# Finishing each attention tile one tile later, three more warm-up runs of TensorE, and a reordered feed-forward tail

## The reference

```
x = x + cross_attention_0(layernorm(x), ctx)      # 16 heads, 16 batches, 1601 keys of width 256
x = x + state_space(layernorm(x), ...)            # gated Mamba-like scan, 16 heads, state 64
x = x + block_ffn(layernorm(x), ...)              # router softmax, top 4 of 16 blocks of 128, relu
x = x + cross_attention_1(layernorm(x), ctx)      # one head: softmax(q k^T) v, 64 queries x 1601 keys a batch
x = x + self_attention(layernorm(x), ...)         # causal, query width 64
x = x + quantised_ffn(layernorm(x), ...)          # weights rounded to 4 bits in blocks of 32

w_block -> s = max(|w_block|) / 7;  clip(round(w / s), -8, 7) * s      # the 4-bit weights
```

## Time and profile before

| | |
|---|---|
| median of 3 runs | 1714.09 us |
| profiled execution, own time / span | 1715.84 / 1714.1 us |
| PE, DVE, ACT, POOL busy | 91%, 68%, 52%, 45% |
| granted TensorE clock, mean | 0.965 of full |
| `state_space` | 851.3 to 993.9 us of the span |
| `block_ffn` | 993.9 to 1229.4 |
| `cross1_queries`, `cross1_batches` | 1229.4 to 1256.7, to 1407.7 |
| `self1`, `quant_ffn` | to the end, not touched |

### The profile page before, as it was taken

One profiled execution on the slowest core, in us unless ns is written; L12 is line 12 of the kernel. 1 busy time (PEld: TensorE's weight loads), 2 busy tenths in 40 slices (PEclk: granted clock), 3 DMA queues, 4 the chain that ended last, 5 costly groups with the idle time before them and its releaser, 6 DMA issues. The chain is left out here.

```text
span 1714.1 us, 33945 instructions
## 1 busy us (share of the span) xinstructions
PE 1559.1 (91%) x13873; PEld 813.7 (47%) x13982; DVE 1167.6 (68%) x1951; ACT 889.2 (52%) x1190; POOL 770.2 (45%) x384
## 2 busy tenths in 40 slices
PE   6999999999999999999799979978878989899469
PEld 3445555555555555555446453333534444444224
DVE  6688888888888888886646448987522233626981
ACT  1487777777777777776373025411211222326750
POOL 1477788888878887885204816642000000000000
PEclk9999999999999999999999969989999999999779
DMA  4589999999999999999713764558679935000001
GB/s 138 131 177 192 193 190 192 190 191 191 194 194 190 199 195 195 189 182 173 166 49 123 232 261 92 140 152 202 196 305 365 396 147 221 1 1 0 1 0 49
DMA packets 556678, 282.74 MB, mean 165 GB/s; under 512 B 482912, under 2 KB 534624, under 8 KB 553456
## 3 DMA queue, kind: packets, MB, share of 16 engines
q1 hardware_dynamic: 556528, 280.63, 69.0%
HBM read 138.74 MB, written 22.54 MB: 94 GB/s over the span
## 5 line engine op out<-in xcount | busy, mean ns | idle before, releaser
L572 POOL TENSOR_TENSOR x<-x_prob,x 128x1604 bf16<-128x1604 f32 x120 | 388.0, 3233 | 142.3 <-ACT x L737 142.3
L867 DVE TENSOR_REDUCE x_negmax<-x_score 128x1 f32<-128x1604 f32 x128 | 233.6, 1825 | 17.3 <-PE x_score L613 7.0
L727 ACT ACTIVATE x_prob<-x_score,x_negmax 128x1604 f32<-128x1604 f32 x128 | 204.8, 1600 | 25.8 <-DVE x_negmax L867 21.1
L596 PE MATMUL x_ring<-x_ctx_hi,wk_split 128*128 128x400 bf16 (+1 forms) x1024 | 216.2, 333 | 0.2 <-DVE x_kT L795 0.2
L596 PE MATMUL x_ring<-wv_split,x_ctx_hi 128*128 128x512 bf16 (+1 forms) x770 | 200.4, 379 | 9.6 <-issue 7.3
L795 DVE SCALAR_TENSOR_TENSOR x_kT<-x_ring,bk,x_kT 128x400 bf16<-128x400 f32 (+1 forms) x256 | 162.2, 634 | 31.8 <-ACT x_kT L716 23.8
L737 ACT CAST x<-x_prob 128x1604 bf16<-128x1604 f32 x120 | 182.9, 1525 | 0.0
L801 DVE TENSOR_TENSOR x_v<-x_ring,x_v 128x512 bf16<-128x512 f32 (+1 forms) x208 | 143.7, 691 | 52.9 <-ACT x_v L720 50.0
L716 ACT ACTIVATE x_kT<-x_ring,bk 128x400 bf16<-128x400 f32 (+1 forms) x196 | 116.3, 594 | 91.0 <-PE x_ring L596 90.0
L720 ACT CAST x_v<-x_ring 128x512 bf16<-128x512 f32 (+1 forms) x148 | 86.5, 585 | 96.8 <-PE x_ring L596 96.8
L596 PEld LDWEIGHTS x_ring<-x_ctx_hi,wk_split 128*128 128x128 bf16 x1024 | 93.9, 97 | 86.9 <-issue 19.7
(11 more groups left out here) (346 smaller groups left out, 2435.9 us busy)
## 6 DMA issues: line engine op xcount, KB each, us to landing
y_ctx<-in_ctx SPq DMA_DIRECT2D x16, 1664.0 KB, 10.4
y_ctxT<-in_ctxT SPq DMA_DIRECT2D x16, 1601.0 KB, 14.3
x_stage<-in_ctxT SPq DMA_DIRECT2D x48, 400.0 KB, 4.4
x_q_rows<-q_rows SPq DMA_DIRECT2D x64, 128.0 KB, 3.2
m_xT<-in_L_ffn_w SPq DMA_DIRECT2D x16, 512.0 KB, 4.5
ffn_w_parts<-m_xT SPq DMA_DIRECT2D x32, 256.0 KB, 2.6
x_stage<-in_ctxT SPq DMA_DIRECT2D x16, 401.0 KB, 5.0
f_w<-ffn_w_parts SPq DMA_DIRECT2D x4, 1024.0 KB, 8.5
```

What stands on the lines that cost most here:

```text
L572: pool.tensor_tensor(ph[:, g % 2, 1, 0:NKP], prob[:, g % 2, :], ph[:, g % 2, 0, 0:NKP], ALU.subtract).then_inc(pl_done, 1)
L596: last = pe.matmul(out_, lhs, rhs, start=(i == 0), stop=(i == len(steps) - 1))
L727: nc.scalar.activation(prob[:, g % 2, :].rearrange("p (c n) -> p c n", n=QW), scores, ACT.Exp, bias=nmax[:, g % 2:g % 2 + 1], accum_out=rs ...
L867: dve.tensor_reduce(nmax[:, pair % 2:pair % 2 + 1], scores, mybir.AxisListType.XY, ALU.max, negate=True).then_inc(max_done, 1)
```

## The change

1. `state_space`: POOL waits for `s_gT` and no longer for all of `s_xo` before it splits weights; 15 identity products stand at the head.
2. `block_ffn`: 20 identity products at the head. The output tiles get eight banks: 0, 1 and the six of the hidden groups. Tiles 2 to 7 wait for the readout of the group that had the bank, the first four tiles for only half of `s_hlo`. `next_weights` stands ahead of the last output tile, and its last product gives a column on all partitions.
3. `Dequant`: the scaling goes from POOL to DVE, where two instructions (subtract and minimum; POOL's product) become one of each kind: `add, min` and `subtract, multiply`. 20 pieces stand in slots 5 to 30, 16 behind, and those are turned one slot after their front.
4. `cross1_queries`: 15 identity products; `cq` becomes a column for each tile by eight small transposes; the `cqs` DMAs go.
5. `cross1_batches`: turning `o`, the product with `wv` and the addition to `x` for tile `u` stand in the step two tiles on, behind that step's scores. The turned `o` has its place in the second half of the bank `pv`.

```
-            pool.wait_ge(s_xo, NT)
+            pool.wait_ge(s_gT, 2 * KD)
...
+            k.keep_busy(pe, ident, banks[7], 15)
...
+        out_banks = banks[0:2] + [hidden_banks[n % 6] for n in range(len(groups) - 6, len(groups))]
+        next_banks = [out_banks[n] for n in range(KD)]
...
-            dq.on_sync(sp, dq.EARLY + 6, late_weights)
+            dq.on_sync(sp, dq.EARLY + 3, late_weights)
...
-                for i in dq.fronts(n):
-                    dq.multiply_on_gpsimd(pool, i)
-            for i in range(dq.EARLY, dq.count):
-                dq.multiply_on_gpsimd(pool, i)
...
+            k.keep_busy(pe, ident, banks[7], 20)
...
-            pe.wait_ge(s_hlo, len(groups))
-            for t in range(NT):
+            def output(t):
                 if t >= 2:
-                    pe.wait_ge(s_out, t - 1)
+                    pe.wait_ge(s_masked, len(groups) - 7 + t)
+                pe.wait_ge(s_hlo, len(groups) if t >= NT // 2 else NB)
...
+            def next_weights():
+                pe.wait_ge(s_late, 48)
+                pe.wait_ge(s_out, KD)
...
+            pe.wait_ge(w2_in, 16)
+            for t in range(NT - 1):
+                output(t)
+            next_weights()
+            output(NT - 1)
...
+            k.keep_busy(pe, ident, banks[2], 15)
             norm.on_tensor(pe)
...
+            pe.wait_ge(s_row, 2)
+            for t in range(NT):
+                last = pe.transpose(banks[6][:, t:t + 1], row[:, P * t:P * t + P], ident[0:1, 0:1])
+            last.then_inc(s_col, 1)
...
-                sp.dma_start(cqs[:, par:par + 1],
-                             cq[:, P * u:P * u + P] if one else cq[:, bass.ds(P * u, P)]).then_inc(cqs_in[par], 16)
...
-            do(NT, NT % 2, False, True)
+            do(NT, NT % 2, False, True, True)
+            do(NT + 1, (NT + 1) % 2, False, False, True)
...
+                if finish:
+                    pe.wait_ge(s_o, u - 1)
+                    for j in range(KC):
+                        last = pe.transpose(pv[:, CD + P * j:CD + P * j + P], o[:, P * j:P * j + P], ident[:])
+                    last.then_inc(s_to, 1)
...
+                if finish:
+                    pe.wait_ge(s_w, 16)
+                    pe.wait_ge(s_of, u - 1)
...
+                        last = pe.matmul(wb[:], oT[:, P * j:P * j + P], wv[:, j, :], start=(j == 0), stop=(j == KC - 1))
+                    last.then_inc(s_wo, 1)
...
-                    pe.wait_ge(s_o, u)
-                    pe.wait_ge(s_tf, 5 * (u - 1) + 3)
...
-    EARLY = 17
+    EARLY = 20
...
-        return self.front_at(i) + 2
+        return self.front_at(i) + (2 if i < self.EARLY else 1)
...
-        dve.tensor_scalar(w, w, ROUND, None, ALU.add).then_inc(self.s_unit, 1)
-        dve.wait_ge(self.s_unit, 6 * i + 5)
-        dve.tensor_scalar(w, w, ROUND, 7.0, ALU.subtract, ALU.min).then_inc(self.s_unit, 1)
...
+        dve.tensor_scalar(w, w, ROUND, ROUND + 7.0, ALU.add, ALU.min).then_inc(self.s_unit, 1)
+        dve.wait_ge(self.s_unit, 5 * i + 5)
+        dve.scalar_tensor_tensor(blocks, blocks, ROUND, s.unsqueeze(2).broadcast_to([P, 512 // QB, QB]),
+                                 ALU.subtract, ALU.mult).then_inc(self.s_back, 1)
```

More of the change, by code:

```diff
@@ L1440, in _ @@
                 for j in range(KD):
[L1441 removed]
+                    last = pe.matmul(out_banks[KD][:, KC:KC + 1], wkb[:, j, CD:CD + 1].broadcast_to([P, P]), bq[:, j:j + 1],
                                      start=(j == 0), stop=(j == KD - 1))
                 last.then_inc(s_next, 1)
[L1444 to L1447 removed]
@@ L1448, in _ @@
-            for j in range(KD):
-                last = pe.matmul(banks[6][0:1, KC:KC + 1], wkb[:, j, CD:CD + 1], bq[:, j:j + 1],
-                                 start=(j == 0), stop=(j == KD - 1))
-            last.then_inc(s_next, 1)
+            pe.wait_ge(w2_in, 16)
[3 more added lines that the diff above has]
+            output(NT - 1)
         @block.scalar
@@ L1743, in each_tile, with tile @@
         def each_tile(eng, do):
-            do(0, 0, True, False)
-            do(1, 1, True, True)
-            with eng.Fori(0, (NT - 2) // 2) as i:
+            do(0, 0, True, False, False)
+            do(1, 1, True, True, False)
+            do(2, 0, True, True, True)
+            do(3, 1, True, True, True)
+            with eng.Fori(0, (NT - 4) // 2) as i:
                 for a in range(2):
-                    do(2 * i + 2 + a, a, True, True)
-            do(NT, NT % 2, False, True)
+                    do(2 * i + 4 + a, a, True, True, True)
+            do(NT, NT % 2, False, True, True)
+            do(NT + 1, (NT + 1) % 2, False, False, True)
         @block.tensor
         def _(pe):
-            def tile(u, par, scores, products):
+            def tile(u, par, scores, products, finish):
+                other = 1 - par
                 if scores:
@@ L1770, in tile, with turn, product @@
                     last.then_inc(s_s, 1)
+                def turn(j):
+                    if j >= 2 or not (isinstance(u, int) and u == 1):
+                        pe.wait_ge(s_tf, 4 * (u - 1) + j - 1)
+                    for i, (k0, kw) in enumerate(TGROUPS[j]):
+                        last = pe.transpose(tb[j % 2][0:kw, P * i:P * i + P], prob[:, other, k0:k0 + kw], ident[:])
+                    last.then_inc(s_t, 1)
+                def product(j):
+                    pe.wait_ge(s_tf, 4 * (u - 1) + j + 1)
+                    for i, (k0, kw) in enumerate(TGROUPS[j]):
+                        for s in range(2):
+                            last = pe.matmul(pv[L * s:L * s + L, 0:CD], pT[0:kw, j, P * i + L * s:P * i + L * s + L],
+                                             cn[0:kw, other, s, 4 * j + i, :],
+                                             start=(j == 0 and i == 0), stop=(j == NTG - 1))
+                    return last
+                if finish:
[3 more added lines that the diff above has]
+                    last.then_inc(s_to, 1)
                 if products:
-                    other = 1 - par
                     n_in = 32 * ((u - 1) // 2 + 1) if isinstance(u, int) else 16 * (u + (1 if par else 0))
@@ L1804, in tile @@
                     product(3).then_inc(s_pv, 1)
-                    pe.wait_ge(s_o, u)
-                    pe.wait_ge(s_tf, 5 * (u - 1) + 3)
-                    for j in range(KC):
-                        last = pe.transpose(tb[other][:, P * j:P * j + P], o[:, P * j:P * j + P], ident[:])
-                    last.then_inc(s_t, 1)
-                    pe.wait_ge(s_tf, 5 * u)
-                    if not (isinstance(u, int) and u == 1):
-                        pe.wait_ge(s_x, u - 1)
-                    for j in range(KC):
-                        last = pe.matmul(wb[:], oT[:, P * j:P * j + P], wv[:, j, :], start=(j == 0), stop=(j == KC - 1))
-                    last.then_inc(s_wo, 1)
             each_tile(pe, tile)
@@ L1820, in _, with tile @@
         def _(act):
-            def tile(u, par, scores, products):
-                other = 1 - par
+            def tile(u, par, scores, products, finish):
                 def turned_back(j):
-                    t = (other + j) % 2
                     n, kw = P * len(TGROUPS[j]), TGROUPS[j][0][1]
-                    act.wait_ge(s_t, 5 * (u - 1) + j + 1)
-                    nc.scalar.copy(pT[0:kw, j, 0:n], tb[t][0:kw, 0:n]).then_inc(s_tf, 1)
+                    act.wait_ge(s_t, 4 * (u - 1) + j + 1)
+                    nc.scalar.copy(pT[0:kw, j, 0:n], tb[j % 2][0:kw, 0:n]).then_inc(s_tf, 1)
+                if finish:
+                    act.wait_ge(s_to, u - 1)
+                    nc.scalar.copy(oT[:], pv[:, CD:CD + KC * P]).then_inc(s_of, 1)
                 if products:
@@ L1839, in tile @@
                     turned_back(3)
-                    act.wait_ge(s_t, 5 * u)
-                    nc.scalar.copy(oT[:], tb[other][:, 0:KC * P]).then_inc(s_tf, 1)
             each_tile(act, tile)
```

116 lines of the change are left out of this document (47 added, 69 removed).

## The result

The changed kernel takes 1700.45 us (median of 15 runs, 1689.74 to 1706.86) against 1714.99 (15 runs, 1712.21 to 1719.06): ratio 0.9912, 95% interval 0.9897 to 0.9927. The forecast was 1682.5, range 1669 to 1697; faster was right, but of the 31.6 us forecast only 14.5 came. The profiled execution took 1699.64 us (span 1697.9), 16.2 less than the one before.

| | forecast | measured | from the rows |
|---|---|---|---|
| `state_space`, head and tail | +6.0 | +5.7 | 993.89 against 988.22 |
| `block_ffn` | +20.5 | +16.0 | 235.5 against 219.5 us |
| `cross1_queries` | +1.4 | +1.7 | 27.4 against 25.7 |
| `cross1_batches` | +3.7 | -4.8 | 150.9 against 155.8 |
| `self1`, `quant_ffn` | 0 | -2.3 | 306.4 against 308.7 |

The account below looks back on a forecast made before the run. No one bound: late weight traffic, PE at the lower clock, full DVE with PE waits, and DMA. Gains 1.8 + 4.2 + 20.5 + 1.4 + 3.7 = 31.6 took 1715.84 to 1684.2, less 1.75: 1682.5 us, range 1669 to 1697.

Parts of the forecast that it names:

- `state_space`, head and tail: Start and end of `state_space`: 1.8 us from identity products, 4.2 of 8.9 open us from POOL's earlier start.
- `cross1_queries`: Whole stage: turns run at the higher clock and `cq` is transposed instead of loaded; 1.4 us gained.
- `cross1_batches`: Whole stage: faster start and a step without finish, partly lost to load order in the loop; 3.7 us gained.
- The head's 1.8 us: Start of `state_space`: fifteen identity products raise the clock, so the fourth copy comes 1.8 us earlier.
- `block_ffn`, head: Norm and router of `block_ffn`: a tile takes 1.3 us instead of 2.45; eight tiles give 9.2 us.
- If the clock is kept: Condition on the 9.2 us in `block_ffn`'s norm and router: PE stays at the higher clock throughout.
- rival 1: Router of `block_ffn`: clock falls after three or four tiles, 5 us lost, 1687.5; with no help 1692; chance 0.25.
- `block_ffn`, behind the head: `block_ffn` after its router: the later of a PE path and a DVE path ends the stage; about 11 us gained.
- Path (b): `block_ffn` after its router: DVE's dequantization pieces set the stage's end, at 1208.9 against 1229.36.
- c: Early dequantization in `block_ffn`: DVE time per piece, taken as 4.5 us, so 20 pieces take 90 us.
- (a): `block_ffn` after its router: PE's path without its waits leads to 1199, the next stage to 1202.
- the ring: `cross1_batches` loop: key and value loads wait on earlier products; two periods take 35.7 us, one 17.85.

Follow-up runs that it names:

- additions_early: Changed kernel with `state_space`'s eight output-bias additions on DVE moved ahead to the gate tiles, before POOL is busy; 1692.8 us, ratio 0.9844.
- changed_again: The changed kernel timed once more without an edit, as the measure for the experiments; 1703.58 us, ratio 0.9899.
- gpsimd_scales: Changed kernel with the dequantization split as before, scale multiplication back on POOL, 20 pieces still early; 1698.74 us, ratio 0.9868.
- router_own_load: Changed kernel where the first router products wait only for the router's matrix, not five small loads; 1697.83 us, ratio 0.9873.
- own_finish: Changed kernel with the finish of each `cross1_batches` tile back in its own step; 1689.2 us, ratio 0.9829.
- router_filled: Changed kernel with the router's matrix on its own load and three identity products behind each router tile; 1689.16 us, ratio 0.9825.
- all_four: Changed kernel with keys issued earlier, the router's own load, identity products behind router tiles, and early `state_space` additions; 1661.62 us, ratio 0.9665.
- filled_only: Changed kernel with three identity products behind each router tile, the router still waiting for five small loads; 1702.79 us, ratio 0.9900.
- fill_key_waits: Changed kernel with 34 identity products on PE ahead of the waits for keys of tiles 3, 5 and 7; 1694.16 us, ratio 0.9862.
- keys_ahead: Changed kernel where SP issues the next tile's keys before waiting to issue the current tile's values; 1678.28 us, ratio 0.9766.

## Why the prediction was wrong

- **`state_space`, +6.0 forecast, +5.7 measured: right**, by its mechanism too: POOL under the additions at +1.0 us each, 5 us of the 8.9 lost again, DVE next in line after 0.30 us. The Trainium skill (GPSIMD Engine Reference, Specifications) names this collision of GpSimd and VectorE; the trace agrees, 1.68 us on average against 0.684, and 0.68 again in additions_early. The head's 1.8 us is not safe: in changed_again PE waited 1.71 us for a load behind the second turned tile and the clock fell there, and in gpsimd_scales behind 1.58; in router_own_load it held behind 1.72.
- **`block_ffn`, head, +9.2 forecast, 0 measured: the step that failed first.** "If the clock is kept" was the condition; it isn't, in most executions. The size was right (own_finish and router_filled show a tile in 1.28 and 1.57 us). The prediction's rival 1 named the router's products as the danger, and router_own_load shows it; the prediction had overlooked that PE also waits for the last of five small loads between the second turned tile and the router. A look at what the first router product waits for, besides `xT`, would have shown it in the code: `s_in` at 80.
- **`block_ffn`, behind the head, +11.3 forecast, +16 measured.** Path (b), the pieces, was put 4.7 us too late. The cost of a piece was right (c = 4.4 for 4.5), but by two errors that cancel: the new last instruction was priced at 1.154 us and takes 0.75 under POOL, and that the rounding ahead of it would go from 0.52 to 0.76, and the small scaling (L2141, now L2148) from 0.37 to 0.50, was not in the sum. The eight additions took 6.4 us and not 9.6, as they too are disturbed less, and the 16 later pieces 1.7 less; only what stands behind the last low part took longer, 10.8 us for 9.1. So (a) and (b) tie with the head slow. With the clock held, PE idles 4.07 (own_finish) or 5.66 us (router_filled) behind its last product instead of 3.08: (b) ends the stage, as forecast, but at 209.9 to 211.7 us and not at 215.0.
- **`cross1_queries`: right** in this execution (+1.7). In changed_again a gap of 4.38 us before it had lost the clock, and the turns took 5.92 us.
- **`cross1_batches`, +3.7 forecast, -4.8 measured: the second step that failed.** That DVE no longer waits for `cqs`, that tile 1's step has no finish, and the ring came as forecast. The clock did not: second scores 7.32 and not 5.6 behind a gap of 4.12 us (1.7), and three scores of 8.21, 8.18 and 7.88 behind waits of 4.2 to 5.4 (2.6, 2.6, 2.3). That is 9.2 us, the whole of the miss of 8.5. The prediction had written down waits of 1.5 to 2 us "ahead of most scores"; they came in every second tile, as 4.2 to 5.4, and it took the clock for safe through them. Its own had a gap of 7.58 that lost it, one of 5.04; nothing in its rows said that 4.1 would not. (A slip in the ring's sum is small beside this: 13.9 + 1.9 + 0.35 makes 16.15, and 15.9 only if the gap of 0.24 is taken off as well; measured are 15.5 us from the scores to the last product at full clock, 18.1 with slow scores.) The Trainium skill (TensorE: Matmul & The Clock Gate, "HAM oscillation") describes such a loop, which falls back to the lower clock at each wait for a DMA; the trace agrees with 8.2 against 5.6 us.
- **The last two stages, -2.3**, aren't touched by the change. In the fourteen profiles of this study they take 305.4 to 309.6 us together, so this lies in the scatter of single executions.

So of the 15 us that are missing in the profiled execution 9 are the router's clock, 9 the loop's and 2 scatter, with 5 given back by the pieces: the waits were forecast about right, and what a wait costs in clock was not. The forecast's middle was also too sure that the clock would hold: rival 1, at 0.25, came true in the head in most executions. With the losses of the loop, which no rival named, the time passed even its 1692 and the top of the range, 1697.

## What to carry to other kernels

Price a wait of PE by its length plus what the work behind it takes at the lower clock, and look for the length of the single wait, not of the mean: here waits of 4.2 to 5.4 us in every second tile each cost 2.3 to 2.6 us more, where 1.5 to 2 in each had been forecast. Before moving work across a wait in a loop, write down SP's issue order beside the events that free each buffer; if a load waits in the queue behind a wait for a later event, moving work can lengthen the period, and here swapping two issues brought 22 us of the stage where the move alone had cost 9. Identity products ahead of a stage gave nothing where the stage's own first products then waited for a load and the clock fell (changed_again), or where the router's 16-column products lost it (router_own_load).

## What was not expected of the hardware

- The clock fell with PE busy without a pause: in router_own_load with the fourth group of turns behind the last gap, 3.9 us on. With three 256-column bfloat16 products to a tile it held (router_filled, all_four), but the same three did not raise it again in 22 us once it was down (filled_only).
- The same code gives different clocks: gaps of 1.16 and 1.14 us (own_finish, fill_key_waits) before the router, and in the first the clock stayed to the end, in the second it fell at the first router tile. This difference is worth 10 us (`block_ffn` 209.9 against 220.5).
- The loads moved 407 GB/s at a DMA share of 0.99 in keys_ahead and 390 at 0.98 before; a share near one did not mean that this loop could not go 12% faster (15.3 us a tile for 17.37), the greater part of it, though, on the lead of two tiles loaded ahead.
